# Two-layer graph network on one core: GpSimd's subtraction waits for the tile's one-hots, its unused constants come later, and no filler matmuls stand between the picks

## The chip, the cores and the metric
The kernel runs on one core of a Trainium2 chip. The core has a matmul engine (TensorE, PE), a vector engine (VectorE, DVE), an activation engine (ScalarE, ACT), a general engine (GpSimd, POOL), and SyncE (SP), whose queue starts the DMAs here. Each engine works through its own list of instructions in order, and semaphores tie the lists together. The metric is the device time of the one launch in microseconds (us); the value of a kernel is the median of its runs.

## The reference
There are 3125 nodes with 256 features and 50000 edges (`src`, `dst`, sorted by `dst`).

```python
# layer 0: mean over the edges of each row, twice, on the same edges
vals  = 1 / max(deg(rows), 1)
neigh = segment_sum(vals[:, None] * x[cols], rows)
x     = relu(concat([x, neigh], 1) @ W.T + b)            # W0,b0 then W1,b1
# outer: x = layernorm(x + two such layers)
# layer 1: the 32 largest of x @ W_neigh are kept per node and averaged over the edges
x     = layernorm(x + (x @ W_self + segment_sum(maxk(x @ W_neigh)[src], dst) / max(deg, 1)[:, None]))
```

Weights, biases and edges are inputs; nothing of them is known when the kernel is built.

## The kernel before, in words
The kernel turns the edge list into a dense matrix C of 3125 x 3125 edge counts, in 25 x 25 blocks of 125 x 125, and then every segment sum is a matmul with C or its transpose.

**Start.** ScalarE turns the edge numbers into floats. VectorE finds the last destination of each chunk of edges (`ends`, helper `whole_part`, L606 and L607), compares it with a ramp (`before`, L621), splits the edge numbers (L625 to L632) and makes selection masks (`pick`, L637). TensorE multiplies the pieces of the edge numbers with the masks in two rounds (k = 0: the first 125 windows, L1385 on `bank`; k = 1: the other 500, L1385 on `pair`). ScalarE copies the results out (`row`, L1089), VectorE unpacks them (L643 to L649), and ScalarE writes them as `jobs` (L1096). GpSimd meanwhile writes the constants: ramps, ones, identities (L483 to L520).

**Tiles 0 and 1.** VectorE compares a ramp with `jobs` and gets one-hot matrices (`hots`, L665, `quick_hots(t, k)`, four sets to a tile). TensorE multiplies them (`fill(t, f)`, L1406), and ScalarE copies the counts into a slab (L1114). In the same stretch the maxima of the weights are found (L688 is the last part), TensorE transposes them (`bounds_t`, L1447), VectorE reduces the transposed rows (`bound_rows`, L772), TensorE turns these once more (`bounds_row`, L1451), and a chain of small VectorE instructions makes scales from them (`bounds`, L784 to L799; `scales_out`, L803). The product of the node features with the weights (`own_product`, L1520) of tile 1 cannot start before the scales.

**The loop over tiles, t = 1 to 24.** For each tile TensorE does the four fills of tile t, the 25 transposes of tile t - 1 (L1486, in groups g = 0 to 3), two products L1520 and two transposes of node features (L1501). VectorE makes the four one-hots of tile t + 1 and copies two of the groups of transposes out of PSUM (`tr_copy`, L822): one-hot 0, group 1, one-hots 1, 2 and 3, group 3. ScalarE copies the fills (L1114), the other two groups (L1153), the transposed features (L1158) and the product (`own`, L1171). Then GpSimd splits the product's half a0 into two 16-bit parts (`split_a0`): a cast (L544, when `own` is there) and a subtraction (L546, when the cast is done). SyncE stores the slab (L353) and half of the product (L360). In tiles 4 and 5 the weights are split as well (L1176 on ScalarE, L817 on VectorE).

**The rest.** From about 172 us on, three series of 625 big matmuls (L1593 twice, L1689) and the dense products (L1494) follow; the change touches nothing there.

`keep_clock(b, n)` (L1349) issues n matmuls of 512 columns on a tile of ones whose result nobody reads. The numbers of a wait on `const_ready` say how many constants must be written: the list of GpSimd sets which ones these are. A path for edge lists that don't fit the windows (`general_...`) is in the program, but not taken with these inputs. It alone reads `iota16`, `woff`, `inc_f`, `rev_f` and `wcol`.

Of the kernel before, what the change touches and what calls it, by code (L numbers as in the profile page):

```python
# [30 lines left out]
NT = N // P  # L31
CH = E // P
# [6 lines left out]
NW = N // W  # L39
# [6 lines left out]
FILLS = len(SETS)  # L46
# [8 lines left out]
KEY = NT * W  # L55
B0W = 13
EQ, EG = 4, CH // 4
# [21 lines left out]
ACT = mybir.ActivationFunctionType  # L79
# [4 lines left out]
def gnn(nc, x, src, dst, w0, b0, w1, b1, wself, wneigh, out):  # L84
    ctx = ExitStack()
    with ctx:
# [174 lines left out]
        const_ready = sem("const_ready")  # L261
# [220 lines left out]
        def _(pool):  # L482
# [16 lines left out]
            for m, n in ((identf, 128), (ident16, PC), (identx, P)):  # L499
# [4 lines left out]
                           allow_small_or_imprecise_dtypes=True).then_inc(const_ready, 1)  # L504
            nc.gpsimd.memset(ones16[:, :], 1.0).then_inc(const_ready, 1)
            nc.gpsimd.memset(epsy[:, :], EPS / YS ** 2).then_inc(const_ready, 1)
            nc.gpsimd.memset(epsb[:, :], EPS).then_inc(const_ready, 1)
            for i in range(2):
# [3 lines left out]
            nc.gpsimd.iota(iota16[:, :], [[1, KEY]], base=0, channel_multiplier=0,  # L512
                           allow_small_or_imprecise_dtypes=True).then_inc(const_ready, 1)
            nc.gpsimd.iota(woff[:, :], [[KEY, NW]], base=0, channel_multiplier=0,
                           allow_small_or_imprecise_dtypes=True).then_inc(const_ready, 1)
            nc.gpsimd.iota(inc_f[:, :], [[1, EQ], [EQ, EG]], base=1, channel_multiplier=0,
                           allow_small_or_imprecise_dtypes=True).then_inc(const_ready, 1)
            nc.gpsimd.iota(rev_f[:, :], [[-1, EQ], [-EQ, EG]], base=CH, channel_multiplier=0,
                           allow_small_or_imprecise_dtypes=True).then_inc(const_ready, 1)
            nc.gpsimd.iota(wcol[:, :], [[0, 1]], base=0, channel_multiplier=1,  # L520
                           allow_small_or_imprecise_dtypes=True).then_inc(const_ready, 1)
            pool.wait_ge(const_ready, 9)
            pool.wait_ge(ws_loaded, 16)
            for c in range(2):
                w_eye = ws_nat[:, c, c * 128:(c + 1) * 128]
                nc.gpsimd.tensor_tensor(w_eye, w_eye, identf[:, :], ALU.add).then_inc(eye_added, 1)

# [7 lines left out]
            def split_a0(t):  # L535

                pool.wait_ge(own_copied, t + 2)
                if t == 0:
                    pool.wait_ge(scale_ready, 1)
                    nc.gpsimd.tensor_tensor(own[:, 0, :], own[:, 0, :], scales[0:P, 1:2].broadcast_to([P, 2 * F]), ALU.mult  # L540
                                            ).then_inc(own_scaled, 1)
                    pool.wait_ge(own_scaled, 1)
                a0 = own[:, t % 2, F:2 * F]
                nc.gpsimd.tensor_copy(xs[:, t, 0:F], a0).then_inc(a0_hi, 1)  # L544
                pool.wait_ge(a0_hi, t + 1)
                nc.gpsimd.tensor_tensor(xs[:, t, F:2 * F], a0, xs[:, t, 0:F], ALU.subtract).then_inc(a0_split, 1)  # L546
# [43 lines left out]
        NCONST = 23  # L590
# [3 lines left out]
        def _(dve):  # L594
# [100 lines left out]
            dve.wait_ge(const_ready, NCONST)  # L695
# [21 lines left out]
            def general_table():  # L717
# [8 lines left out]
                dve.wait_ge(win_hot, 2 * FILLS)  # L726
                dve.wait_ge(win_done, FILLS)
# [176 lines left out]
            with dve.If(total > E - 1):  # L904
                for t in range(1, NT):
# [3 lines left out]
                    if t == 1:  # L909
                        bound_rows()  # L910
                    if t == 2:
                        dve.wait_ge(cols_copied, 4)
# [141 lines left out]
        def _(act):  # L1054
# [7 lines left out]

            def as_float(j, n):
                a.activation(edges_f[:, j], edges_i[:, j], ACT.Copy).then_inc(floats_ready, 1)
                act.wait_ge(floats_ready, n)
# [112 lines left out]
            def quick_copies():  # L1178
                quick_copy(0, FILLS - 1)
                square_x(3)  # L1180
                for t in range(1, NT):
                    own = OWN[t]
                    quick_copy(t, 0)
                    if t == 1:
                        own_t(0)
                    tr_copy(t - 1, 0)
# [157 lines left out]
        def _(pe):  # L1344
# [30 lines left out]
            for k, (lo, hi) in enumerate(PICKS):  # L1375
                for blk in range(2):
                    out = both[1][:, blk, 0:hi - lo] if k else bank[4][:, blk * hi:(blk + 1) * hi]
                    mm(out, ones_row[:, :], minus_row[:, lo:hi], start=True, stop=False, skip_group_check=True)
                    for g in range(EQ):
# [7 lines left out]
                        if k:  # L1387
                            keep_clock(bank[7], 1)
# [350 lines left out]
```

## Time and profile before
| | us |
|---|---|
| median of 3 runs (lowest, highest) | 659.98 (658.75, 664.8) |
| profiled execution, its own time | 660.82 |
| its span in the profile | 659.0 |
| TensorE busy in the span | 632.4 (96%) |
| VectorE busy | 494.8 (75%) |
| ScalarE busy | 315.4 (48%) |
| GpSimd busy | 111.4 (17%) |
| mean granted TensorE clock | 0.989 of 2.4 GHz |

A busy share is a mean over the whole span, and stages differ: VectorE is busy without a break in the loop over tiles and half idle later on. Times of instructions are counted from the start of the span. An instruction's end is drawn until its result is written, so the next one on the engine can start some 0.1 us before it.

### The profile page before, as it was taken

How to read it: one execution, taken by the hardware profiler on the slowest of the kernel's cores; microseconds unless marked ns; L12 is line 12 of the kernel's file. 1: busy time of each engine (PE TensorE's matmuls, PEld its weight loads, DVE VectorE, ACT ScalarE, POOL GpSimd, SP SyncE). 2: the span in 40 equal slices, each digit the busy share in tenths (PEclk: the TensorE clock that was granted, in tenths of full speed). 3: DMA queues.
4: the chain of work that ended last, by engine and by line, in shares of the span. 5: the costliest groups of instructions: out<-in, count | busy, mean ns of one | idle time of the engine just before them, and what ended most of it. 6: DMA issues, size and time to landing. Idle time of an engine off the chain costs nothing.

```text
span 659.0 us, 10805 instructions
## 1 busy us (share of the span) xinstructions
PE 632.4 (96%) x3758; PEld 322.7 (49%) x3759; DVE 494.8 (75%) x1273; ACT 315.4 (48%) x606; POOL 111.4 (17%) x188
## 2 busy tenths in 40 slices
PE   8879999999999999999998999999999999999996
PEld 3456666776544444444443444444444444444442
DVE  7888999999759998888845588878878837533333
ACT  3678999999397777676622222222222200000000
POOL 3104221221200111001002223232232200000000
PEclk9979999999999999999999999999999999999999
DMA  8534655555522222222224999999999533300000
GB/s 212 109 97 141 225 178 184 186 172 172 160 42 64 59 69 67 53 61 58 51 52 133 189 182 201 180 185 196 174 202 177 154 99 116 111 26 26 24 24 24
DMA packets 66742, 79.62 MB, mean 121 GB/s; under 512 B 30320, under 2 KB 59407, under 8 KB 66681
## 3 DMA queue, kind: packets, MB, share of 16 engines
q1 hardware_dynamic: 66681, 78.86, 55.5%
q8 instruction: 32, 0.52, 0.4%
q14 instruction: 29, 0.24, 0.1%
HBM read 38.91 MB, written 33.38 MB: 110 GB/s over the span
## 4 chain that ended last, share of the span: by engine, by line
PE 63%; DVE 22%; DMA 6%; ACT 4%; POOL 3%; issue 2%; SPq 0%; ACTq 0%; DVEq 0%; POOLq 0%
PE pair L1593 21%; PE bank L1689 11%; PE pair L1689 10%; PE bank L1520 5%; DVE hots L665 4%; PE bank L1486 4%; DMA tr_sb<-part 4%; PE pair L1406 4%; DVE m L985 3%; PE bank L1494 3%; PE pair L1494 3%; DVE work L990 3%; ACT a L1273 2%; POOL part L573 2%; DVE ct L822 1%
## 5 line engine op out<-in xcount | busy, mean ns | idle before, releaser
L1593 PE MATMUL pair<-a,ct 125*128 125x512 f16 x625 | 139.5, 380 | 0.0
L1593 PE MATMUL pair<-xs,ct 125*128 125x512 f16 x625 | 139.1, 379 | 0.0
L665 DVE TENSOR_TENSOR hots<-iota,jobs 125x1792 f16<-125x1792 f16 (+1 forms) x100 | 103.7, 1073 | 0.7 <-ACT jobs L1096 0.7
L1593 PEld LDWEIGHTS pair<-a,ct 125*128 125x128 f16 x625 | 62.3, 100 | 74.6 <-issue 1.4
L1593 PEld LDWEIGHTS pair<-xs,ct 125*128 125x128 f16 x625 | 61.9, 99 | 72.5
L1114 ACT ACTIVATE slab<-pair 125x875 f16<-125x875 f32 (+1 forms) x100 | 83.3, 860 | 3.3 <-PE pair L1406 1.7
L1273 ACT ACTIVATE a<-ct 125x1000 f16<-125x1000 f16 (+1 forms) x75 | 80.4, 1072 | 1.6
L555 POOL TENSOR_TENSOR own_in<-own_in,bias_sb 125x256 f32<-125x256 f32 x50 | 37.6, 752 | 238.5 <-DMA own_in<-own_dram 238.4
L1689 PE MATMUL bank<-xs,ct 125*128 125x512 f16 (+1 forms) x325 | 71.5, 379 | 0.0
L1689 PE MATMUL pair<-xs,ct 125*128 125x512 f16 x300 | 66.2, 379 | 0.0
L1340 ACT ACTIVATE sd<-mv,epsb 125x1 f32<-125x1 f32 x25 | 7.4, 294 | 113.9 <-DVE mv L1047 113.9
L878 DVE SCALAR_TENSOR_TENSOR t<-pair,rdeg,own_in 125x256 f32<-125x256 f32 x50 | 24.1, 482 | 48.0 <-PE pair L1593 43.3
L1486 PEld LDWEIGHTS bank<-ident,slab 125*128 125x128 f16 x625 | 39.6, 99 | 35.9 <-issue 22.1
L1486 PE MATMUL bank<-ident,slab 125*128 125x125 f16 x625 | 51.5, 220 | 4.8 <-ACT slab L1114 1.7
L1406 PE MATMUL pair<-hots 125*128 125x125 f16 x625 | 52.4, 223 | 3.9 <-DVE hots L665 3.0
L1520 PE MATMUL bank<-w_t,x_t 128*125 128x512 f32 x100 | 53.6, 621 | 1.6 <-DVE sv L784 0.9
L1689 PEld LDWEIGHTS bank<-xs,ct 125*128 125x128 f16 (+1 forms) x325 | 32.3, 99 | 37.9
L1689 PEld LDWEIGHTS pair<-xs,ct 125*128 125x128 f16 x300 | 29.9, 100 | 34.9
L1406 PEld LDWEIGHTS pair<-hots 125*128 125x128 f16 x625 | 40.6, 100 | 7.7 <-issue 4.7
L1494 PE MATMUL bank<-w_lay,tr_sb 128*128 128x512 f16 x150 | 37.6, 388 | 4.2 <-DMA tr_sb<-part 4.2
L822 DVE COPY ct<-bank 125x1008 f16<-125x1008 f16 x50 | 33.7, 673 | 7.6 <-PE bank L1486 7.6
L856 DVE TENSOR_TENSOR tree<-tree,ct 125x630 uint16<-125x630 uint16 x75 | 37.5, 500 | 1.8
(203 smaller groups left out, 753.7 us busy)
## 6 DMA issues: line engine op xcount, KB each, us to landing
c_dram<-slab SPq DMA_DIRECT2D x25, 683.6 KB
ct<-c_dram SPq DMA_DIRECT2D x25, 683.6 KB
own_in<-own_dram SPq DMA_DIRECT2D x50, 125.0 KB
own_dram<-own SPq DMA_DIRECT2D x25, 125.0 KB
own_dram<-own_st SPq DMA_DIRECT2D x25, 125.0 KB
x_in<-in_x_dram SPq DMA_DIRECT2D x25, 125.0 KB
z_dram<-z_st SPq DMA_DIRECT2D x25, 125.0 KB
a<-z_dram SPq DMA_DIRECT2D x5, 625.0 KB
```

The costliest lines, as they stand in the source:

```text
L555: nc.gpsimd.tensor_tensor(own_in[k % 2][:, :], own_in[k % 2][:, :], bias_sb[:, :], ALU.add).then_inc(own_biased, 1)
L665: v.tensor_tensor(hots[k][:, :, :, :].rearrange("p w g (a d) -> p (w g) a d", d=2), iota, job, ALU.is_equal).then_inc(win_hot, 1)
L822: v.tensor_copy(ct[:, TG0[g]:TG0[g] + TG[g], t, :], tr16[1][0:P, 0:TG[g], 0:PC]).then_inc(tr_free[1], 1)
L856: step(v.tensor_tensor(tree[:, :], tree[:, :], quint[k], ALU.add))
L1114: a.activation(slab3[t % 2][:, :, lo * QW:hi * QW].rearrange("p b (w d) -> p b w d", d=QW), pair[f % 2][0:P, 0:n, 0:QKEY].rearrange("p w ( ...
L1273: a.activation(unread[:, 0:(hi - lo) * P].rearrange("p (b s) -> p b s", s=P), ct[:, lo:hi, T, 0:P], ACT.Copy, accum_out=deg_part[:, T, k:k ...
L1406: last = mm(pair[f % 2][:, u, 0:QKEY], hots[f][:, u, 0, :], hots[f][:, u, 1, 1:QKEY + 1], start=True, stop=True, skip_group_check=True)
L1486: last = nc.tensor.transpose(tr16[g % 2][:, i, 0:P], slab[par][:, (TG0[g] + i) * P:(TG0[g] + i) * P + 128], ident16[:, 0:P])
L1494: last = mm(out, lhs(2 * pt + h), w[:, h, q, :], start=h == 0 and k == 0, stop=h == 1 and k == 2, skip_group_check=True)
L1520: last = mm(bank[6][0:P, :].rearrange("p (a f) -> p a f", a=2), x_t32[:, h, :], w0_t[:, h::2, :], start=h == 0, stop=h == 1, skip_group_ch ...
L1593: ins = mm(agg[k % 3][0:lhs.shape[1], :], lhs, parts[l][:, t, :], start=t == 0, stop=t == NT - 1, skip_group_check=True)
L1689: ins = mm(out3[T % 8][0:lhs.shape[1], :], lhs, xs[:, b, :], start=b == 0, stop=b == NT - 1, skip_group_check=True)
```

## The change
GpSimd's list of constants is cut in three. The first eleven that count for `const_ready` stay where they were. Seven short ones wait until VectorE has written `row_key` and `row_src` of the first round (`cols_ready` 2). The five that only the general path reads wait until the one-hots of tiles 0 and 1 are done (`win_hot` 8) and count for a semaphore of their own. VectorE's first one-hot waits for 11 constants instead of 23. The two addends of identities (L526 before, L516 now) keep their wait for the weights. In `split_a0` the subtraction of tiles 4 to 23 waits for the four one-hots of tile t + 1. The eight matmuls of ones between the picks of round k = 1 are gone. ScalarE runs one activation of a single element at its start.

```diff
@@ gpsimd
             nc.gpsimd.iota(iota128[:, :], ...).then_inc(const_ready, 1)
+            pool.wait_ge(cols_ready, 2)
             nc.gpsimd.memset(ones16[:, :], 1.0).then_inc(const_ready, 1)
...
             nc.gpsimd.memset(onesq[:, :], 1.0).then_inc(const_ready, 1)
-            nc.gpsimd.iota(iota16[:, :], ...).then_inc(const_ready, 1)
-            nc.gpsimd.iota(woff[:, :], ...).then_inc(const_ready, 1)
-            nc.gpsimd.iota(inc_f[:, :], ...).then_inc(const_ready, 1)
-            nc.gpsimd.iota(rev_f[:, :], ...).then_inc(const_ready, 1)
-            nc.gpsimd.iota(wcol[:, :], ...).then_inc(const_ready, 1)
-            pool.wait_ge(const_ready, 9)
             pool.wait_ge(ws_loaded, 16)
             for c in range(2):
                 w_eye = ws_nat[:, c, c * 128:(c + 1) * 128]
                 nc.gpsimd.tensor_tensor(w_eye, w_eye, identf[:, :], ALU.add).then_inc(eye_added, 1)
+            pool.wait_ge(win_hot, 2 * FILLS)
+            nc.gpsimd.iota(wcol[:, :], ...).then_inc(general_ready, 1)
+            nc.gpsimd.iota(iota16[:, :], ...).then_inc(general_ready, 1)
+            nc.gpsimd.iota(woff[:, :], ...).then_inc(general_ready, 1)
+            nc.gpsimd.iota(inc_f[:, :], ...).then_inc(general_ready, 1)
+            nc.gpsimd.iota(rev_f[:, :], ...).then_inc(general_ready, 1)
@@ split_a0
                 pool.wait_ge(a0_hi, t + 1)
+                if 3 < t < NT - 1:
+                    pool.wait_ge(win_hot, FILLS * (t + 2))
                 nc.gpsimd.tensor_tensor(xs[:, t, F:2 * F], a0, xs[:, t, 0:F], ALU.subtract).then_inc(a0_split, 1)
@@
-        NCONST = 23
+        NCONST = 18
@@ vector
-            dve.wait_ge(const_ready, NCONST)
+            dve.wait_ge(const_ready, 11)
...
                     if t == 1:
                         bound_rows()
+                        dve.wait_ge(general_ready, 5)
@@ scalar
+            act.wait_ge(warm_ready, 1)
+            a.activation(own[0:1, 0, 0:1], warm[0:1, 0:1], ACT.Copy)
...
                     if t == 1:
                         own_t(0)
+                        act.wait_ge(general_ready, 5)
@@ tensor, picks
-                        if k:
-                            keep_clock(bank[7], 1)
```

GpSimd's list before, from the ramp that the one-hots read (`iota`, L503) to the first split; the names after the numbers of lines are the tiles written and read:

```order
L503 IOTA iota_66 125x128
L505 MEMSET ones_52 125x1
L506 MEMSET epsy 125x1
...
L511 MEMSET onesq 125x125
L512 IOTA iota_86 125x625
L514 IOTA woff 125x125
L516 IOTA inc_f 125x400
L518 IOTA rev_f 125x400
L520 IOTA wcol 125x1
L526 TENSOR_TENSOR ws_nat<-ws_nat,identf 128x128 [waits ws_loaded,const_ready]
```

The same place now:

```order
L503 IOTA iota_66 125x128
L506 MEMSET ones_52 125x1 [waits cols_ready]
L507 MEMSET epsy 125x1
...
L512 MEMSET onesq 125x125
L516 TENSOR_TENSOR ws_nat<-ws_nat,identf 128x128 [waits ws_loaded]
L516 TENSOR_TENSOR ws_nat<-ws_nat,identf 128x128
L518 IOTA wcol 125x1 [waits win_hot]
L520 IOTA iota_86 125x625
L522 IOTA woff 125x125
L524 IOTA inc_f 125x400
L526 IOTA rev_f 125x400
```

The stretch behind the ramp starts only when VectorE has unpacked the first round, and the five general constants have moved behind the addends and behind tile 1's one-hots.

VectorE's list now, from tile 1's last one-hots into the loop's first pass:

```order
L668 TENSOR_TENSOR hots_64<-iota_66,jobs 125x1536 [waits win_done]
L688 TENSOR_REDUCE stat<-bcol 128x2 [waits b_loaded]
L691 TENSOR_REDUCE stat<-ws_nat 128x2 [waits eye_added]
...
L668 TENSOR_TENSOR hots_61<-iota_66,jobs 125x1792 [waits win_done]
L777 TENSOR_REDUCE stat_r<-bank 16x1 [waits stat_psum]
L778 TENSOR_REDUCE stat_r<-bank 16x1
L827 COPY ct<-bank 125x8x126 [waits tr_done,general_ready]
```

VectorE's order is the old one. New is the wait for `general_ready` ahead of the first copy of transposes, and that GpSimd's five constants now start when the first of these rows ends.

TensorE's second round of picks now:

```order
L1388 MATMUL pair<-minus_row,ones_row 128x500
L1395 MATMUL pair<-pick,quint 128x500
L1395 MATMUL pair<-pick,piece 128x500 x2
L1395 MATMUL pair<-pick,quint 128x500
L1395 MATMUL pair<-pick,piece 128x500 x2
```

Before, a row `L1349 MATMUL bank<-warm 128x512` stood behind each pair of `quint` and `piece` rows of this round, eight in all.

## Rows read from the trace of the kernel before
**Rows 1.** Stretches: length, busy us of each engine (instructions), granted clock, DMA

```profile
34.40:40.00 5.60, 5.09 (x46) 4.48 (x47) 3.72 (x8) 4.65 (x8) 0.00 (x0) 0.50 0.44 141
40.00:48.00 8.00, 6.20 (x65) 4.51 (x64) 7.52 (x24) 5.98 (x11) 0.04 (x1) 0.99 0.34 101
...
78.00:125.00 47.00, 45.94 (x505) 32.47 (x504) 47.00 (x55) 44.90 (x73) 10.37 (x18) 1.00 0.56 174
...
370.00:600.00 230.00, 226.63 (x1046) 102.33 (x1044) 164.08 (x564) 48.39 (x131) 45.81 (x68) 1.00 0.87 151
```

**Rows 2.** Timeline, start: start us, us, engine, line, operation, tiles [idle <-releaser]

```profile
4.07 0.24 POOL L503 IOTA iota<- 125x128 f16 x1
...
4.18 2.32 DVE L606 TENSOR_SCALAR ends<-ends 100x4 f32<-100x4 f32 x1
...
4.29 1.28 ACT L1064 ACT_TABLE_LOAD   x1 [4.15 <-DMA edges_i<-in_dst_dram]
...
4.73 0.65 POOL L512 IOTA iota<- 125x625 f16 x1
...
6.41 0.13 POOL L520 IOTA wcol<- 125x1 f32 x1
6.53 0.17 DVE L607 TENSOR_SCALAR ends<-ends 100x4 f32<-100x4 f32 x1
6.73 1.91 DVE L621 TENSOR_SCALAR before<-win_row,ends 100x625 f16<-100x625 f32 x4
```

**Rows 3.** Chain that ended last, second round of picks: start us, us, what

```profile
17.88 0.43 PE bank L1349
...
20.55 0.22 PE bank L1349
...
25.28 1.11 ACT row L1089
```

**Rows 4.** Timeline, tiles 0 and 1

```profile
26.41 1.20 DVE L643 SCALAR_TENSOR_TENSOR held_row<-row 125x1000 f32<-125x1000 f32 x1 [1.49 <-ACT row L1089]
...
32.97 1.80 DVE L665 TENSOR_TENSOR hots<-iota,jobs 125x1536 f16<-125x1536 f16 x2
...
35.38 1.09 DVE L665 TENSOR_TENSOR hots<-iota,jobs 125x1792 f16<-125x1792 f16 x1
...
36.85 0.27 DVE L773 TENSOR_REDUCE stat_r<-bank 16x1 f32<-16x128 f32 x1
...
37.59 0.21 PE L1451 MATMUL bank<-identf,stat_r 16*1 16x16 f32 x2
```

**Rows 5.** Timeline, one pass of the loop

```profile
103.43 1.07 PE L1520 MATMUL bank<-w_t,x_t 128*125 128x512 f32 x2
...
104.62 0.60 PE L1486 MATMUL bank<-ident,slab 125*128 125x125 f16 x8
...
105.33 0.40 POOL L544 CAST xs<-own 125x256 f16<-125x256 f32 x1 [4.00 <-ACT own L1171]
105.39 0.67 DVE L822 COPY ct<-bank 125x1008 f16<-125x1008 f16 x1
105.48 0.38 ACT L1158 ACTIVATE x_t<-bank 128x250 f32<-128x250 f32 x1 [0.21 <-PE bank L1501]
...
105.81 0.67 POOL L546 TENSOR_TENSOR xs<-own,xs 125x256 f16<-125x256 f32 x1
...
105.99 1.31 DVE L665 TENSOR_TENSOR hots<-iota,jobs 125x1536 f16<-125x1536 f16 x1
...
108.08 0.95 DVE L665 TENSOR_TENSOR hots<-iota,jobs 125x1536 f16<-125x1536 f16 x1
```

**Rows 6.** Timeline of GpSimd's casts and a store's wait in the loop

```profile
73.56 0.90 POOL L544 CAST xs<-own 125x256 f16<-125x256 f32 x1 [4.83 <-ACT own L1171]
...
87.38 0.93 ACT L1114 ACTIVATE slab<-pair 125x875 f16<-125x875 f32 x1 [0.43 <-DMA c_dram<-slab]
...
167.41 0.40 POOL L544 CAST xs<-own 125x256 f16<-125x256 f32 x1 [4.00 <-ACT own L1171]
```

More of the change, by code:

```diff
@@ L258, in gnn @@
         out3 = [bank[i] for i in (7, 2, 0, 1, 5, 6, 3, 4)]
-        const_ready = sem("const_ready")
+        const_ready, general_ready = sem("const_ready"), sem("general_ready")
         src_loaded, dst_loaded, dst_more = sem("src_loaded"), sem("dst_loaded"), sem("dst_more")
@@ L511, in _ @@
             nc.gpsimd.memset(onesq[:, :], 1.0).then_inc(const_ready, 1)
[L512 to L521, printed above, removed]
-            pool.wait_ge(const_ready, 9)
             pool.wait_ge(ws_loaded, 16)
@@ L526, in _ @@
                 nc.gpsimd.tensor_tensor(w_eye, w_eye, identf[:, :], ALU.add).then_inc(eye_added, 1)
+            pool.wait_ge(win_hot, 2 * FILLS)
+            nc.gpsimd.iota(wcol[:, :], [[0, 1]], base=0, channel_multiplier=1,
+                           allow_small_or_imprecise_dtypes=True).then_inc(general_ready, 1)
+            nc.gpsimd.iota(iota16[:, :], [[1, KEY]], base=0, channel_multiplier=0,
+                           allow_small_or_imprecise_dtypes=True).then_inc(general_ready, 1)
+            nc.gpsimd.iota(woff[:, :], [[KEY, NW]], base=0, channel_multiplier=0,
+                           allow_small_or_imprecise_dtypes=True).then_inc(general_ready, 1)
+            nc.gpsimd.iota(inc_f[:, :], [[1, EQ], [EQ, EG]], base=1, channel_multiplier=0,
+                           allow_small_or_imprecise_dtypes=True).then_inc(general_ready, 1)
+            nc.gpsimd.iota(rev_f[:, :], [[-1, EQ], [-EQ, EG]], base=CH, channel_multiplier=0,
+                           allow_small_or_imprecise_dtypes=True).then_inc(general_ready, 1)
             steps = [3]
@@ L726, in general_table @@
                 dve.wait_ge(win_hot, 2 * FILLS)
+                dve.wait_ge(general_ready, 5)
+                dve.sem_inc(win_hot, FILLS * NT)
                 dve.wait_ge(win_done, FILLS)
@@ L910, in _ @@
                         bound_rows()
+                        dve.wait_ge(general_ready, 5)
                     if t == 2:
```

## The prediction
> **What bounds the kernel now.** I read the page first, then the stretches, then the timelines of the stretches that the change touches. TensorE is busy 96% of the span, but that is a mean. From 370 us on it is busy 226.63 of 230 us and nothing there is changed [rows 1]. So the change can only move the moment at which the series of big matmuls begins, and whatever it moves there reaches the end in full. Ahead of it lie two stages with other limits.
>
> In the start a chain runs from the edge list through VectorE, TensorE's two rounds of picks and VectorE again. The odd row is L606: 2.32 us for 100x4 elements, where L607, the same kind on the same tile, takes 0.17. L606 ends at 6.50, and GpSimd, which issued constants without a break, ends its last one at 6.54 [rows 2]. So VectorE was held until GpSimd stopped.
>
> In the loop over tiles VectorE is busy 47.00 of 47.00 us, ScalarE 44.90 [rows 1]. VectorE binds. One of its four one-hots takes 1.31 us where an equal one takes 0.95: 0.36 more. It starts at 105.99 beside GpSimd's subtraction, which runs from 105.81 to 106.48 and keeps its 0.67 [rows 5]. The cast at 105.33 lies beside VectorE's copy out of PSUM, and neither is stretched. A pass takes (167.41 - 73.56) / 18 = 5.21 us [rows 6].
>
> **Constants out of the early chain.** GpSimd's last instruction ahead of its new wait is the ramp of L503, which ends at 4.31 [rows 2]. L606 then ends about there, L607 runs 4.36 to 4.53, and L621 can start at 4.56 instead of 6.73: 2.17 us earlier. Bounds: 0, if something else held L606, and 2.2, if it is not held at all. I take 2.17, as the two ends coincide within 0.04. What follows is VectorE's own work up to the picks, so the shift holds. The seven short constants now come after `row_src` of the first round, while VectorE waits for ScalarE's `jobs`; they lay between 4.31 and 4.73 before [rows 2], so 0.4 us at most; beside a wait I put nothing. VectorE's first one-hot waits for fewer constants: nothing, they were long there. ScalarE's table load, 1.28 us from 4.29 [rows 2], moves ahead of the edges' arrival; VectorE wants the first floats after L621's 1.91 us, in the changed kernel at 6.47, 0.9 us after the table load's old end at 5.57, and then works on the first for three instructions; nothing either.
>
> **The ones between the picks.** Eight matmuls at 0.43 each, as the first, are 3.4 us; at 0.22, as a later one [rows 3], 1.8. The clock rises early in the round, so I take 2.1 us on the chain. They can't bring all of it. VectorE reads the second round's copy at 26.41 after 1.49 us of idleness, so it was ready at 24.92 [rows 4]; 2.17 earlier that is 22.75. TensorE's side gives 25.28 - 2.17 - 2.10 = 21.0, with the copy's 1.11 then 22.1. VectorE is late by then, and L643 starts at 22.75: 26.41 - 22.75 = 3.66 us for both edits together. The bounds are 2.17 (the ones bring nothing) and 4.27 (all of both).
>
> **General constants after tile 1's one-hots.** These last one-hots end at 34.77 [rows 4], less 3.66 is 31.11. GpSimd then works from about 31.17 through its five constants, 6.54 - 4.73 = 1.81 us [rows 2], to 32.98. VectorE wants the next one-hot (before at 35.38, so at 31.72) and is held as at L606: 1.26 us. The two reductions behind it, which ended at 37.12, would be awaited at 37.59 [rows 4], by TensorE's L1451; they had 0.17 us of idleness before them and 0.47 behind. 1.26 - 0.17 - 0.47 = 0.6 us late, on the chain to the scales. Bounds: 0, and 1.26. The new waits for `general_ready` on VectorE and ScalarE come later than 32.98 and cost nothing. So the loop is entered 3.66 - 0.6 = 3.06 us earlier.
>
> **The subtraction.** It now starts when the fourth one-hot ends, which is about 0.08 after VectorE's copy (group 3) has started; with the wait's 0.06 it runs from 0.14 to 0.81 of that copy. The next one-hot follows 0.60 after a copy's start [rows 5]. So 0.2 us of overlap is left instead of 0.49. 0.49 cost 0.36, 0.13 less than the overlap, so 0.2 costs 0.05 to 0.09. VectorE's pass loses about 0.3 us. Behind it stand the others. TensorE's eight transposes start at 104.62, 0.12 after the product's drawn end at 104.50; they waited for VectorE's copy, and ScalarE's L1158 idled 0.21 for TensorE [rows 5]. ScalarE's idle time is (47.00 - 44.90) / 9 = 0.23 us to a pass [rows 1]. With VectorE 0.3 faster ScalarE and TensorE's order become the limit, and I take 0.23 us to a pass, with ends at 0.12 and 0.31. 18 passes: 4.1 us (2.2 to 5.6). Queued behind the waiting subtraction is only the next tile's cast, some 1.4 us later; ScalarE's `own` waits for the subtraction two tiles back. Both are free. Tiles 4 and 5 are bound by ScalarE, which also splits weights there; nothing.
>
> **Sum.** 3.06 + 4.1 = 7.2 us. Against the profiled execution's own time of 660.82 that is 653.6; the median of the runs is 0.84 lower, so **652.8**. The terms' bounds give 650.3 to 655.6 for this case.
>
> **Rivals.** (1) *The loop is bound elsewhere already.* Once ScalarE waited 0.43 us in it for a slab's store to land [rows 6]; if stores or ScalarE's order take over at once, 0.05 us or less to a pass is left: 3.06 + 0.9, 656. Against it: only one such wait in 18 passes. (2) *The low clock stays.* The first of the ones took 0.43, a later one 0.22 [rows 3]: the granted clock rose from 1.2 to 2.4 GHz during this dense round, after TensorE had waited for VectorE. With nothing between the picks it could rise only later. 26 matmuls at 0.43 are 11.2 us from 13.9, to 25.1: 0.2 us instead of 3.66, and a gain of 0.2 - 0.6 + 4.1 = 3.7, 656.3. Against it: the picks are back to back, so TensorE is no less busy without the ones. After the branch the clock was 0.50 for 5.6 us, and 0.99 in the next 8 with 6.20 us of work [rows 1]; where it falls there shifts the entry by up to 1 us either way. The Trainium skill (TensorE: Matmul & The Clock Gate, What's actually happening) says that the gate is closed by default and that activity opens it. By that rule filler between dense matmuls adds no activity, and the first term stays; the rise in the trace inside the dense round agrees. (3) *Slower: the subtraction holds the copy.* In its new place it lies beside a copy out of PSUM for 0.45 us; the trace shows one only where the first copy's last 0.25 us runs beside it (105.81 against 106.06 [rows 5]). If each copy is held for the full 0.67, a pass changes by 0.67 - 0.36 = +0.31, 5.6 us in all, less 3.06: +2.5, 662.5. It decides from 0.53 us to a pass on. Against it: the cast beside the copy stretches nothing. The Trainium skill (GPSIMD Reference, Specifications) names contention for VectorE instructions in a 2-port mode or with two SBUF inputs; the copy reads PSUM, so by that rule it isn't held, the one-hot with two SBUF inputs is, and the sum is mine. No row here shows a whole subtraction beside a copy. (4) *L606 was not held by GpSimd*, the edit doesn't do what it says: then 1.49 (VectorE's idleness, filled by the ones' 2.1) - 0.6 + 4.1 = 5.0, 655.
>
> **Chances.** Forecast 0.60; (1) 0.13; (2) 0.10; (3) 0.04; (4) 0.05; both terms at their upper ends or more, 650 or below, 0.08. The range reaches from the lower bound to (2): 650.0 to 656.5. A change of 1% is about what can be told from none: 653.4 and 666.6 are the lines. The forecast lies only 0.6 us inside the first, so I put six tenths of its chance below, with the last case 0.44, and 0.03 more for a low clock that falls away altogether: faster 0.47, within 1% 0.50, slower 0.03.
>
> **What would show it.** L606 at about 0.2 us and L621 starting at 4.6. L643 of the second round at 22.8 with no or little idle time before it. Five constants at 31 to 33 and a one-hot of 2 us or more beside them. In the loop, four one-hots of 1.08 and 0.95 us, the subtraction beside a copy of unchanged 0.67, a pass of 4.98, and ScalarE without idle time before L1158. L1520's products after the scales 3.1 us earlier. It is wrong if the loop's pass stays at 5.15 or more, if the clock is low for longer in the first 50 us, or if TensorE waits anew after the branch.

## The result, and the profile after

| | before | after |
|---|---|---|
| median of 4 runs, us (lowest, highest) | 660.53 (658.75, 664.8) | 652.61 (652.33, 653.37) |
| ratio, 95% interval | | 0.9882 (0.9842 to 0.9923) |
| profiled execution, its own time | 660.82 | 652.5 |
| its span | 659.0 | 650.7 |
| TensorE, VectorE, ScalarE busy | 632.4, 494.8, 315.4 | 624.4, 487.2, 314.8 |

The forecast was 652.8. The change makes the kernel 1.2% faster, with an interval that reaches from 0.8% to 1.6%. The medians differ by 7.92 us. The profiled executions differ by 8.32 us. Three instants cut this sum: the cast of tile 6 comes 3.85 us earlier (73.56 to 69.71), the 18 passes behind it take 3.99 us less, and 0.48 us is gained behind the cast of tile 24. That last piece is within the scatter: from this cast to the end the profiles of the network kernels below take 490.3 to 492.0 us, with the same instructions there.

The timeline of the changed kernel's start answers [rows 2]; L609, L610 and L624 are L606, L607 and L621 of before.

```profile
4.07 0.24 POOL L503 IOTA iota<- 125x128 f16 x1
4.18 0.17 DVE L609 TENSOR_SCALAR ends<-ends 100x4 f32<-100x4 f32 x1
4.39 0.17 DVE L610 TENSOR_SCALAR ends<-ends 100x4 f32<-100x4 f32 x1
4.59 1.91 DVE L624 TENSOR_SCALAR before<-win_row,ends 100x625 f16<-100x625 f32 x4
```

The instruction that took 2.32 us takes 0.17, and L624 starts 2.14 us earlier.

The next rows, from the timelines of GpSimd, ScalarE, VectorE and TensorE, answer [rows 4]. L646 is L643 of before, L668 is L665, L1459 is L1451.

```profile
19.97 1.10 ACT L1098 ACTIVATE row<-pair,shift 125x1000 f32<-125x1000 f32 x1 [0.84 <-PE pair L1395]
22.49 1.19 DVE L646 SCALAR_TENSOR_TENSOR held_row<-row 125x1000 f32<-125x1000 f32 x1
...
31.01 0.67 POOL L520 IOTA iota<- 125x625 f16 x1
31.47 1.09 DVE L668 TENSOR_TENSOR hots<-iota,jobs 125x1792 f16<-125x1792 f16 x1
32.27 0.48 POOL L526 IOTA rev_f<- 125x400 f32 x1
...
33.66 0.21 PE L1459 MATMUL bank<-identf,stat_r 16*1 16x16 f32 x2
```

ScalarE's row copy comes 5.31 us earlier and VectorE's L646 3.92, now without idle time. The ramps for the general path run from 31.01 to 32.75, beside the whole of the one-hot at 31.47, and it takes 1.09 us as before. L1459 is 3.93 us earlier: nothing was given back between the two.

The stretches of the changed kernel, in the columns of [rows 1]: the picks, the branch, the work behind it, the loop, and the matmuls at the end.

```profile
13.90:19.80 5.90, 5.90 (x29) 2.48 (x28) 4.89 (x13) 4.32 (x7) 0.82 (x8) 1.00 1.14 218
28.00:30.00 2.00, 0.00 (x0) 0.00 (x0) 2.00 (x5) 0.34 (x2) 0.00 (x0) 0.63 0.00 0
30.00:36.00 6.00, 5.02 (x49) 4.34 (x49) 4.06 (x8) 5.05 (x8) 1.83 (x5) 0.55 0.42 132
...
78.00:125.00 47.00, 46.33 (x525) 34.28 (x525) 46.77 (x57) 46.20 (x76) 11.81 (x20) 1.00 0.60 188
361.70:591.70 230.00, 226.66 (x1048) 103.02 (x1046) 164.43 (x565) 48.28 (x131) 45.88 (x68) 1.00 0.84 151
```

The picks run at the full granted clock, where the kernel before had 0.51 from 16.2 to 19.6, in these rows of its timeline and stretches:

```profile
13.92 0.21 PE L1385 MATMUL bank<-pick,quint 100*128 100x125 f16 x1 [1.13 <-DVE pick L637]
...
16.20:19.60 3.40, 3.40 (x9) 1.18 (x9) 2.44 (x7) 3.40 (x6) 0.67 (x2) 0.51 1.13 256
```

Behind the branch the clock is at 1.2 GHz as before. In the loop ScalarE went from 44.90 of 47.00 us to 46.20, and VectorE from 47.00 to 46.77. TensorE's busy time at the end is that of before, 226.66.

One pass of the loop, and behind the dots the casts of tiles 6 and 24 and a copy between them, from the timelines of the engines, answer [rows 5] and [rows 6].

```profile
98.08 0.67 DVE L827 COPY ct<-bank 125x1008 f16<-125x1008 f16 x1
98.30 0.67 POOL L549 TENSOR_TENSOR xs<-own,xs 125x256 f16<-125x256 f32 x1 [2.73 <-DVE hots L668]
98.67 1.25 DVE L668 TENSOR_TENSOR hots<-iota,jobs 125x1792 f16<-125x1792 f16 x1
...
100.43 2.68 DVE L668 TENSOR_TENSOR hots<-iota,jobs 125x1536 f16<-125x1536 f16 x3
...
69.71 0.40 POOL L545 CAST xs<-own 125x256 f16<-125x256 f32 x1 [1.45 <-ACT own L1180]
82.70 0.93 ACT L1123 ACTIVATE slab<-pair 125x875 f16<-125x875 f32 x1 [0.69 <-DMA c_dram<-slab]
159.57 0.40 POOL L545 CAST xs<-own 125x256 f16<-125x256 f32 x1 [0.97 <-ACT own L1180]
```

The subtraction lies beside the copy for 0.45 us, and the copy keeps its 0.67. The subtraction's last 0.30 us lies beside the next one-hot, which takes 1.25. The other three take 2.68 together. A pass is (159.57 - 69.71) / 18 = 4.99 us.

### The profile page after: what moved, and what is told of

The parts are those of the page before. It is cut to its first block, busy times and chain, and to the rows that moved or that the text cites. A ratio compares the mean times of both kernels' runs of the same rounds, so it can differ in the third digit from the quotient of the medians.

```text
span 650.7 us, 10811 instructions
## 1 busy us (share of the span) xinstructions
PE 624.4 (96%) x3750; PEld 322.3 (50%) x3751; DVE 487.2 (75%) x1273; ACT 314.8 (48%) x607; POOL 111.3 (17%) x188
## 4 chain that ended last, share of the span: by engine, by line
PE 50%; DVE 19%; ACT 17%; DMA 5%; issue 4%; POOL 3%; SPq 0%; ACTq 0%; DVEq 0%; POOLq 0%
PE pair L1601 21%; PE bank L1697 11%; PE pair L1697 10%; ACT slab L1123 8%; DVE m L991 4%; DVE work L996 3%; PE bank L1502 3%; DMA tr_sb<-part 3%; PE pair L1502 3%; ACT ct L1162 2%; POOL part L576 2%; ACT own L1180 2%; ACT a L1283 2%; DVE hots L668 2%; POOL xs L580 1%
## 5 line engine op out<-in xcount | busy, mean ns | idle before, releaser
L668 DVE TENSOR_TENSOR hots<-iota,jobs 125x1792 f16<-125x1792 f16 (+1 forms) x100 | 99.0, 1025 | 0.8 <-ACT jobs L1105 0.8
```

What stands on the lines that cost most here:

```text
L668: v.tensor_tensor(hots[k][:, :, :, :].rearrange("p w g (a d) -> p (w g) a d", d=2), iota, job, ALU.is_equal).then_inc(win_hot, 1)
```

## Experiments

Times are medians. A ratio is to the kernel before, in runs on the same chip. "Cast 0", "cast 6" and "cast 24" are GpSimd's casts of these tiles; before they start at 49.07, 73.56 and 167.41.

### The three parts, each alone

**e1_consts**: the kernel before with only the constants moved, and the waits on them that go with it.

```diff
+            pool.wait_ge(cols_ready, 2)
             nc.gpsimd.memset(ones16[:, :], 1.0).then_inc(const_ready, 1)
...
-            nc.gpsimd.iota(iota16[:, :], ...)   # and woff, inc_f, rev_f, wcol
...
+            pool.wait_ge(win_hot, 2 * FILLS)
+            nc.gpsimd.iota(iota16[:, :], ...).then_inc(general_ready, 1)   # and the other four
```

> The kernel before with the constants' move alone (the ones between the picks and the old subtraction stay). Theory A, GpSimd's stream of constants holds L606: L606 takes 0.17 us instead of 2.32, the chain to the second picks moves by 2.2 us, VectorE still idles for the picks, and the launch gains 2.2 us, 1.9 to 2.6 (about 658 against 660.5). Theory B, L606 is slow by itself and the start's gain of the full change came from the ones: L606 stays at 2.3, gain 0 to 0.3. For the five general constants: if they hold the one-hot beside them, that one-hot takes 2 us or more and the gain is only 1.6; the changed kernel's trace speaks for 1.09 us and no loss.

Measured: 657.7, ratio 0.9963 (0.9944 to 0.9982). L607 (L606 before) takes 0.17 us at 4.18. Rows of ScalarE's, VectorE's and GpSimd's timelines and the stretch of the picks:

```profile
21.51 1.10 ACT L1092 ACTIVATE row<-pair,shift 125x1000 f32<-125x1000 f32 x1 [3.00 <-PE pair L1389]
22.64 1.20 DVE L644 SCALAR_TENSOR_TENSOR held_row<-row 125x1000 f32<-125x1000 f32 x1
45.39 1.15 POOL L545 CAST xs<-own 125x256 f16<-125x256 f32 x1
...
13.90:21.60 7.70, 7.70 (x39) 3.30 (x37) 6.69 (x15) 4.41 (x8) 2.23 (x9) 1.00 1.13 225
```

With the ones still between the picks, cast 0 comes 3.68 us earlier. Of the 3.66 that I had shared out between the constants and the ones, the constants alone bring all: the clock does not fall in the picks any more, and VectorE's 1.49 us of idleness goes with that. Theory A had L606 right and this wrong: it expected VectorE to go on idling. The medians differ by 2.34 us, as expected, but the profiled executions by 3.58. The 3.68 us are those of the profiles, and how many of the other executions have them is not shown.

**e2_ones**: the kernel before with only the ones taken out.

```diff
-                        if k:
-                            keep_clock(bank[7], 1)
```

> The kernel before without the eight matmuls of ones, nothing else changed. Theory A: TensorE ends the second picks 1.8 to 2.1 us earlier, VectorE's idle time of 1.49 us before L643 vanishes and bounds the gain: 1.4 to 1.5 us. Theory B, without the ones the granted clock stays at 1.2 GHz for longer: the picks of 500 columns take 0.43 us to the end and the gain is 0 or a loss of up to 2 us. Theory C, the picks gain all of 2.1.

Measured: 660.07 (657.11 to 665.17), ratio 0.9991 (0.9964 to 1.0019).

```profile
16.20:25.30 9.10, 9.10 (x22) 2.92 (x22) 6.84 (x15) 4.02 (x7) 0.93 (x2) 0.50 0.80 176
...
4.39 3.78 DVE L621 TENSOR_SCALAR before<-win_row,ends 100x625 f16<-100x625 f32 x4
26.48 1.10 ACT L1089 ACTIVATE row<-pair,shift 125x1000 f32<-125x1000 f32 x1 [6.26 <-PE pair L1385]
27.61 1.20 DVE L643 SCALAR_TENSOR_TENSOR held_row<-row 125x1000 f32<-125x1000 f32 x1 [3.33 <-ACT row L1089]
51.70 1.15 POOL L544 CAST xs<-own 125x256 f16<-125x256 f32 x1
```

This is my rival (2), on its own. TensorE is busy for all of the 9.10 us, and the granted clock is 0.50 throughout: VectorE waits 3.33 us instead of 1.49, and cast 0 is 2.63 us late. The profiled execution took 662.6, 2.5 more than the median, so not every execution pays this much. But no gain was found either. One more reading: L606 began 0.24 us earlier here (3.94) and took 0.21, L607 took its 0.17 at 4.18, and the hold fell on L621, 3.78 us for 1.91. So the hold is tied to no single instruction, and to no single instant either: at 4.18 L606 was held in the kernel before, and L607 was not held here.

**e3_sub**: the kernel before with only the subtraction's wait.

```diff
                 pool.wait_ge(a0_hi, t + 1)
+                if 3 < t < NT - 1:
+                    pool.wait_ge(win_hot, FILLS * (t + 2))
```

> The kernel before with the subtraction's wait alone. Theory A: a pass of the loop takes 4.96 to 5.0 us instead of 5.21, 18 passes bring 3.9 to 4.1 us, the launch gains 4 (about 656.5). The one-hot behind the copy keeps 0.17 us of stretch. Theory B, the loop's gain needed an earlier start (other landings of the stores): under 3 us, with ScalarE waiting for stores more than once. If the three parts are independent, their gains (2.2, 1.5, 4.0) add up to 7.7 against 7.9 measured for all.

Measured: 655.41, ratio 0.9925 (0.9896 to 0.9953).

```profile
73.14 0.40 POOL L544 CAST xs<-own 125x256 f16<-125x256 f32 x1 [1.44 <-ACT own L1174]
162.62 0.40 POOL L544 CAST xs<-own 125x256 f16<-125x256 f32 x1 [1.02 <-ACT own L1174]
```

A pass is 4.97 us instead of 5.21. Cast 6 is 0.42 earlier, and so is cast 0 by 0.41, ahead of the first tile that the edit touches, so that this is scatter of the start. The whole gain of the loop comes from this wait. The product of the ratios of e1 and e3 is 0.9888, that of the full change 0.9882.

### What GpSimd's work does to VectorE's

**m1_table** leaves the network out and runs groups of four VectorE instructions beside eight of GpSimd's.

> Not the network: only a table of what GpSimd's work does to VectorE's. Five kinds of VectorE work, four of each back to back (scalar on 32-bit data, comparison of two 16-bit tiles as in the one-hots, copy out of PSUM, reduction, three-operand instruction with two SBUF inputs) stand beside five of GpSimd's (nothing, ramps, memsets, casts, subtractions, eight of each back to back). Theory A, one lock for everything: each of VectorE's SBUF kinds is held by each of GpSimd's until its stream ends. Theory B, it depends on the pair: ramps and memsets, which only write, hold the one-input scalar kind (L606) but not the comparison (0.95 us stays), while the subtraction, which reads, holds the comparison (0.3 us or more each); the copy out of PSUM and the reduction are held by none (0.67 stays). The changed kernel's trace speaks for B: its one-hot beside the ramps took 1.09.

The rows are VectorE's timeline. The order is: beside nothing (from 4.21), beside ramps (17.64, 24.01), beside subtractions (from 92.85).

```profile
4.21 1.67 DVE L73 TENSOR_SCALAR d_ts<-a 125x625 f32<-125x625 f32 x4 [0.16 <-POOLq L88]
6.04 3.56 DVE L75 TENSOR_TENSOR d_eq<-iota,jobs 125x1536 f16<-125x1536 f16 x4 [0.15 <-POOLq L93]
...
17.64 3.20 DVE L73 TENSOR_SCALAR d_ts<-a 125x625 f32<-125x625 f32 x4 [0.15 <-POOLq L93]
24.01 3.56 DVE L75 TENSOR_TENSOR d_eq<-iota,jobs 125x1536 f16<-125x1536 f16 x4 [3.17 <-POOLq L108]
...
92.85 4.98 DVE L75 TENSOR_TENSOR d_eq<-iota,jobs 125x1536 f16<-125x1536 f16 x4 [3.20 <-POOLq L108]
101.04 2.45 DVE L77 COPY d_cp<-ps 125x1008 f16<-125x1008 f16 x4 [3.21 <-POOLq L108]
```

All of it, in us for four:

| VectorE | alone | ramps | memsets | casts | subtractions |
|---|---|---|---|---|---|
| scalar, one SBUF input | 1.67 | 3.20 | 3.27 | 2.27 | 3.09 |
| one-hot, two SBUF inputs | 3.56 | 3.56 | 3.56 | 4.16 | 4.98 |
| three-operand, two SBUF inputs | 2.50 | 2.50 | 2.50 | 3.09 | 3.92 |
| copy out of PSUM | 2.45 | 2.45 | 2.45 | 2.45 | 2.45 |
| reduction | 2.47 | 2.46 | 2.46 | 2.46 | 2.46 |

So ramps and memsets, which read nothing, hold the scalar kind alone; casts and subtractions hold also what has two SBUF inputs; copies out of PSUM and reductions are never held. The Trainium skill (SBUF — State Buffer, SBUF: two separate sides) gives a rule for it: the two engines share one pair of ports as a lock, which a VectorE instruction with two SBUF inputs contends for only against a GpSimd operation that reads SBUF. The table agrees in both rows with two SBUF inputs.

**d4_more**: the kernel before with four more ramps of 400 in front of its general constants.

```diff
+            nc.gpsimd.iota(cover[:, :], [[1, CH]], ...)   # and cover2, cover3, cover4
             nc.gpsimd.iota(iota16[:, :], ...)
```

> The kernel before with four more ramps of 400 (0.47 us each, 1.9 in all) on GpSimd right ahead of its general constants. Theory A (VectorE's one-input instruction is held until GpSimd's stream of constants ends): L606, 2.32 us before, grows by as much as the stream, to 4.1 to 4.3, and L607 starts near 8.4 instead of 6.53. Theory B (a fixed cost at the start, or a hold by the first constants alone): L606 stays at 2.3. If its edges land 0.2 earlier the hold may fall on L621 instead.

Measured: 660.45 in its one run.

```profile
4.18 4.00 DVE L614 TENSOR_SCALAR ends<-ends 100x4 f32<-100x4 f32 x1
8.11 0.13 POOL L528 IOTA wcol<- 125x1 f32 x1
...
8.00:14.00 6.00, 4.98 (x16) 2.06 (x17) 5.76 (x13) 0.86 (x3) 0.24 (x2) 0.72 1.13 238
14.00:25.30 11.30, 11.30 (x73) 5.90 (x72) 10.29 (x22) 6.52 (x11) 0.93 (x2) 1.00 1.03 198
```

The first instruction (L614 is L606) grows with the stream, from 2.32 to 4.00, and the stream by 1.70: the hold is GpSimd's doing. What I had not foreseen is the rest. With VectorE 1.68 us later from there on, the second round's unpacking starts at 26.47 against 26.41, and cast 0 at 49.16 against 49.07. The clock is low from 10.2 to 13.7 us, ahead of the picks, and full in them. So in this profile the hold was 1.7 us longer for nothing: what set the end of the start in the kernel before was the low clock in the picks.

### TensorE's clock

**d3_moved** asks whether the second round needs its ones, or only a TensorE that was busy ahead of it. The 8 ones go, and 4 stand in the first round, where TensorE waits for VectorE (the expectation miscounts them as 10 and 5, and so does that of c2_onesback).

```diff
-                        if k:
-                            keep_clock(bank[7], 1)
+                        if k == 0 and blk == 0:
+                            keep_clock(bank[3], 1)
```

> The kernel before with the 10 multiplications of ones taken out of the second round of picks and 5 put into the first, one behind each group of three in its first block, where TensorE waits for VectorE's pick. The constants stay early and no wait is added. Theory A (the clock falls at 16.2 because TensorE worked only 2.14 of the 3.4 us before it, and the second round needs no ones once it has the full clock): clock 1.00 from 14 to 25, ScalarE's row copy of the second round 3 us or more earlier than 25.28, L643 at 22.6 to 24, cast of tile 0 near 45.4 to 47. Theory B (the second round itself loses the clock without its ones, as in e2_ones): clock 0.50 from 16 or 20 on, row copy after 25, cast of tile 0 at 49 or later. Kernel: A 656 to 658, B 660 to 661.

Measured: 658.24, ratio 0.9971 (0.9951 to 0.9991).

```profile
22.51 1.09 ACT L1089 ACTIVATE row<-pair,shift 125x1000 f32<-125x1000 f32 x1 [1.71 <-PE pair L1385]
49.43 1.15 POOL L544 CAST xs<-own 125x256 f16<-125x256 f32 x1
...
24.00:46.00 22.00, 15.25 (x122) 10.75 (x120) 18.30 (x40) 14.61 (x23) 0.00 (x0) 0.69 0.24 76
```

Theory A holds for the picks: the second round runs at full clock (1.00 from 14 to 30) without ones of its own, and the row copy is 2.77 us earlier than in [rows 3]. L643, at 25.21, is 1.20 earlier, short of the 22.6 to 24 that was expected. Theory A's cast 0 was missed: the clock was low from 30.2 to 43.8, where before it was from 33.4 to 40.2, and that took the 1.20 back; the four products L1520 in front of cast 0 took 3.78 us, 1.98 before. The profiled execution was the slowest of the ten (660.07), so most of them need not have had this; the median lies between what the two theories expected.

**c2_onesback**: the changed kernel with the 8 ones put back.

> The changed kernel with the multiplications of ones put back after each group of three in the second round of picks (10 of 0.22 us). Theory A (with the earlier constants' move the clock does not fall any more, and the ones are worth only what the kernel with the constants' move alone shows, 0.16 us at tile 0's cast): ScalarE's row copy moves from 19.97 to about 21.5, VectorE's L648 (the second round's first instruction) from 22.49 to 22.6, cast of tile 0 from 45.23 to 45.4, kernel 652.5 to 653.2. Theory B (my prediction's reason, the ones are 2.1 us on the chain of which 1.5 is a gain at L646): cast of tile 0 moves by over 1 us, kernel 653.8 or more.

Measured: 653.25, ratio 0.9889 (0.9836 to 0.9942); L646 at 22.64 and cast 0 at 45.39, 0.15 and 0.16 us later than without the ones. In the changed kernel they are nearly free: ScalarE's copy ends at 21.07 there, 1.4 us before VectorE wants it, and with the ones just in time. This kernel has ScalarE's early activation and e1_consts has not, and cast 0 is at 45.39 in both, so that the early table load brings nothing there, as predicted.

**c3_filler**: the changed kernel with ones on TensorE behind the product of the hits, where it waits for the branch.

```diff
             last.then_inc(counted, 1)
+            pe.wait_ge(wt_copied, 4)
+            keep_clock(bank[7], 8)
```

> The changed kernel with 8 multiplications of ones (8 of 0.21 us on TensorE) right behind the product of the hits, where TensorE is idle from 27.5 to 30.5 while VectorE copies the match and the engines read it; the granted clock is 0.67 in the idle stretch and near 0.5 from 30.4 to 36. Theory A (the clock fell because TensorE stood idle there, and work in its place keeps it): granted clock near 1.00 from 28 to 34, the transposes L1494 and the picks of tile 1 run at about half their duration, and cast of tile 0 comes 0.3 to 1.0 us earlier than 45.23. Theory B (the work behind 30.5 is itself too sparse): clock low all the same from 31 on, cast of tile 0 within 0.15 us of 45.23. If the 8 delay TensorE's reading of the match, cast of tile 0 is up to 0.5 us later. The kernel's time: 651.6 to 652.9.

Measured: 651.03 (650.48 to 651.67), ratio 0.9851 (0.9798 to 0.9903).

```profile
27.21 0.24 PE L1428 MATMUL bank<-onesq,hits 125*1 125x1 f32 x4 [2.42 <-DVE hits L658]
27.38 3.48 PE L1359 MATMUL bank<-warm 128*128 128x512 f16 x8
...
29.00:30.00 1.00, 1.00 (x4) 0.39 (x3) 1.00 (x4) 0.06 (x1) 0.00 (x0) 0.50 0.00 0
31.00:32.00 1.00, 0.48 (x7) 0.24 (x4) 1.00 (x2) 1.00 (x1) 1.00 (x4) 1.00 0.57 171
44.26 1.15 POOL L545 CAST xs<-own 125x256 f16<-125x256 f32 x1
```

The eight took 3.48 us, as the clock had fallen as they began, after 2.42 us of idleness; it was back at 1.00 by 31 us, and cast 0 came 0.97 us earlier than in the changed kernel. That is theory A's cast 0. But the ones did not keep the clock, as it had it: they brought it back 4.7 us sooner (at 30.6 for 35.4).

**d1_fill2** puts eight ones ahead of the product too, and both eights into a bank that is free then. **d2_best** adds the gate of c4_eyegate.

```diff
+            pe.wait_ge(win_read, FILLS - 1)
+            keep_clock(bank[0], 8)
             pe.wait_ge(count_ready, 2)
...
             last.then_inc(counted, 1)
+            keep_clock(bank[0], 8)
```

> The changed kernel with 16 multiplications of ones into a bank of pair 0 that is free then: 8 ahead of the product of the hits (once ScalarE has read tile 0's third set, near 25.5; TensorE was idle from 24.8 to 27.2) and 8 behind it. In c3_filler the clock fell at 27.3, before its 8 ones began, so they only brought it back at 30.7. Theory A (the clock falls because TensorE stands idle from 24.8 on): with work from 25.5 it stays at 1.00 through 27 to 30, the 16 take 0.21 us each, and the changed kernel's low stretch of 28 to 34.7 is gone; cast of tile 0 at 44.0 to 44.3 (45.23 in the changed kernel, 44.26 in c3_filler), since from 30.7 on both have the full clock; kernel 650.5 to 651.5. Theory B (the gap of 0.7 us and the 1.5 us at the branch are enough to lose it): the clock falls near 28 to 31 again and the cast is at 44.3 to 45.3.

> d1_fill2 and the gate of c4_eyegate together: the pair of one-hots beside the additions falls from 2.08 to 1.82 and VectorE's chain to the second one-hots (no idle in it) is 0.26 shorter. Theory A: cast of tile 0 0.1 to 0.3 us earlier than in d1_fill2. Theory B (ScalarE's wait for the data xs, which was 0.76, 1.17 and less in the runs so far, decides when the first one-hots start and swamps it): no difference beyond 0.4 either way. Kernel 650.2 to 651.5.

Measured: d1 652.15, ratio 0.9893 (0.9864 to 0.9921); d2 652.32, ratio 0.9887 (0.9857 to 0.9917). Two stretches of d1 and one of d2:

```profile
24.00:33.00 9.00, 6.17 (x48) 3.30 (x45) 8.71 (x16) 6.72 (x11) 1.83 (x5) 1.00 0.18 52
33.00:36.00 3.00, 3.00 (x33) 2.71 (x30) 1.61 (x3) 2.46 (x6) 0.00 (x0) 0.50 0.36 127
...
24.00:46.00 22.00, 17.07 (x158) 11.02 (x156) 20.25 (x46) 17.21 (x28) 4.72 (x8) 1.00 0.29 90
```

In d1 the clock survives the branch and falls at 33, which neither theory had; cast 0 is at 44.79, in theory B's range and outside theory A's. In d2 the clock never falls, and cast 0 is at 44.07, the earliest of all and 0.72 before d1's, more than either theory allowed. Both medians lie above what was expected. The two programs differ only in GpSimd's gate. In d2 ScalarE also waited 1.11 us for a load of `xs` ahead of the first eight, in d1 0.29, so that they ran from 25.96 and from 24.99. From 29 to 33 TensorE was then busy for 2.54 us in d2 and for 1.79 in d1. So I can't put the kept clock down to the edit. The table sets the stretch from the second round's unpacking to cast 0 beside the mean granted clock from 24 to 46 us.

| kernel | L643 or L646 | cast 0 | between | clock 24 to 46 |
|---|---|---|---|---|
| d2_best | 22.27 | 44.07 | 21.80 | 1.00 |
| c3_filler | 22.45 | 44.26 | 21.81 | 0.92 |
| d1_fill2 | 22.55 | 44.79 | 22.24 | 0.92 |
| before | 26.41 | 49.07 | 22.66 | 0.84 |
| after | 22.49 | 45.23 | 22.74 | 0.84 |
| e1_consts | 22.64 | 45.39 | 22.75 | 0.84 |
| d4_more | 26.47 | 49.16 | 22.69 | 0.84 |
| d3_moved | 25.21 | 49.43 | 24.22 | 0.69 |

VectorE's and ScalarE's work between the two is the same in all eight but for what GpSimd's work adds, and the stretch follows the clock: 2.4 us from the best to the worst. The other kernels fit: e2_ones took 24.09 us at 0.73, and e3_sub, c1_nosub, c2_onesback and c4_eyegate 22.68 to 22.75 at 0.84.

Against the changed kernel nothing of this is settled by time. c3's ratio to the kernel before is 0.9851 with an interval that holds 0.9882, and those of d1 and d2 are 0.9893 and 0.9887. A gain of 1 us is 0.15%, less than these intervals can tell. What the traces show is an earlier cast 0.

### The rest of the loop and of the start

**c1_nosub**: the changed kernel without the subtraction in tiles 4 to 23.

```diff
+                if 3 < t < NT - 1:
+                    pool.sem_inc(a0_split, 1)
+                else:
                     nc.gpsimd.tensor_tensor(xs[:, t, F:2 * F], ...)
...
```

> This is the changed kernel without the subtraction of tiles 4 to 23 on GpSimd; the first layer's aggregates of those tiles read tile 0's halves instead (that part of the result is left out), and no other instruction is missing. It asks what the 0.17 us that still lie on the one-hot behind the copy (1.25 us there, 1.08 free) cost. Theory A (ScalarE sets the pass now: 89.06 us busy of 89.86 in 18 passes, and VectorE has slack): the pass stays at 4.93 to 4.99 us, the one-hot falls to 1.08, cast of tile 24 within 1 us of 159.57, kernel 651.5 to 652.7. Theory B (VectorE still sets it and the residual stretch is paid): the pass falls by 0.17 to about 4.82, cast of tile 24 near 156.5, kernel near 649.5. The two differ at 156.5 against 159.

Measured: 654.46 (653.41 to 661.05), ratio 0.992 (0.9889 to 0.9952).

```profile
69.94 0.40 POOL L545 CAST xs<-own 125x256 f16<-125x256 f32 x1 [5.62 <-ACT own L1183]
98.31 1.07 DVE L671 TENSOR_TENSOR hots<-iota,jobs 125x1792 f16<-125x1792 f16 x1
159.63 0.40 POOL L545 CAST xs<-own 125x256 f16<-125x256 f32 x1 [5.10 <-ACT own L1183]
```

The one-hot is at its free 1.07 us, and a pass takes 4.98 us all the same. So the 0.17 us that the subtraction still takes from VectorE costs nothing: theory A, VectorE does not set the pass. In the 18 passes ScalarE is busy for 88.74 of 89.69 us and VectorE for 87.66, which points at ScalarE. The median, though, is 1.8 us above what theory A expected, while the profiled execution (653.41) has the stretch behind cast 24 as the others; where the rest went no trace shows. What moves the mean pass now is ScalarE's wait for a slab's store. c2_onesback had three such waits in its loop (0.74, 0.80 and 0.84 us) and a mean pass of 5.07; d2_best had none, and 4.97.

**c4_eyegate**: GpSimd's two additions wait for tile 0's last one-hots.

```diff
+            pool.wait_ge(win_hot, FILLS)
             for c in range(2):
                 w_eye = ws_nat[:, c, c * 128:(c + 1) * 128]
```

> The changed kernel with GpSimd's two additions to the weights (L516, 2.21 us at 19.48) held until tile 0's last one-hots are done (21.3). Now they lie beside two one-hots of VectorE (2.08 us against 1.82 for such a pair). Theory A (reading work of GpSimd holds one-hots and two-input instructions but no reductions): the pair of one-hots falls to 1.82, L646 starts near 22.23 (0.26 earlier) if nothing else holds it; of the additions most lies beside the reductions L679 and L683 (0.67 each, unchanged), and a remainder may stretch L646 (1.19) by up to 0.2. Cast of tile 0 0.1 to 0.3 us earlier than 45.23. Theory B (the stretch of the one-hots is no matter, since ScalarE's L1113 and its row copy set the time): L646 and the cast unmoved within 0.05. The kernel's time stays within 0.5 us either way.

Measured: 653.95, ratio 0.9899 (0.9847 to 0.9951). The pair of one-hots falls from 2.08 to 1.82, as theory A had it. Yet L647 (L646 before) starts at 22.67, 0.18 later: the first one-hots waited 1.16 us for ScalarE's `jobs` instead of 0.75, ScalarE having waited 0.30 us for a load of `xs` that had not held it in the changed kernel. One profile can't part the two. The median is 1.3 us above the changed kernel's, outside the 0.5 that was expected. In d2_best, with the same gate, L647 is at 22.27, 0.28 earlier than in d1_fill2.

## Why the prediction was right, point by point

**L606.** Right: 2.14 us for 2.17, and d4_more shows that GpSimd's stream is the cause.

**The ones, and the entry into the loop.** The size was right: 3.66 predicted for both edits, 3.92 measured at L646. The working was not. I wrote that the ones were 2.1 us on the chain and so filled VectorE's 1.49 us of idleness. e1_consts has the ones and none of the idleness, c2_onesback puts the ones' worth at 0.15 us, and e2_ones has neither ones nor gain. What made the 1.49 was the clock. In the kernel before, TensorE waited 1.13 us for VectorE's first pick, was busy for 2.14 us in all between 12.8 and 16.2, the clock fell then, and the round ran at 0.51 until 19.6. With the constants out of the way VectorE's picks come 2.1 us earlier, TensorE waits 0.23 us for them (e1_consts) or not at all, and the clock stays. The profiles bear this out together: the three kernels with that wait of 1.13 us and nothing in its place (before, e2_ones, e3_sub) lose the clock between 15 and 17 us, and all eight with the constants moved have 1.00 from 8 to 28 us, c3_filler to 27. d3_moved fills the wait and keeps the clock as well. In d4_more the picks come last of all and run at full clock, as TensorE had its low stretch before them; so what counts is not when the picks come. I had read the clock as rising in the round, which it does, and had not asked why it was low at its start. Of the further 0.26, 0.20 is from GpSimd's additions: before they lay beside the first pair of one-hots (2.42 us for 1.96), after beside the second (2.08 for 1.82). That the size came out is luck: both terms were bounded by the same idle time, so the sum was the same whichever of them earned it.

**The general constants.** This step failed: "VectorE wants the next one-hot [...] and is held as at L606". It was put at 0.6 us and cost none. m1_table says why: a ramp reads nothing, and a one-hot beside it keeps its 3.56. I had taken the price from a scalar instruction, which is of another kind.

**The subtraction.** Right: 4.99 us for a pass, 4.98 predicted, and 3.99 us for the 18 against 4.1. The residual on the one-hot is 0.17, not 0.05 to 0.09, but by c1_nosub it is hidden: VectorE is no longer the limit. The step that named the next limit, ScalarE and TensorE's order, held that far; which of the two it is was not tested.

**The sum.** 7.2 predicted, 8.32 in the profiles: 0.8 more at the entry (0.6 that did not occur, and the 0.26), 0.1 less in the loop, and 0.5 behind it, which is scatter. The forecast of 652.8 lies 0.2 from the median although the sum is 1.1 short, because I took 0.84 off between the profiled execution and the median, and for the changed kernel the median lies 0.1 above. That closeness is luck. The stated bounds of 650.3 to 655.6 are also not quite those of the terms: with 1.26 us lost on the general constants the slow end is 659.98 - (2.17 - 1.26 + 2.2), 656.9. Nothing hung on it.

**The rivals.** (1), the loop bound elsewhere, is true only beyond 4.98. (2), the low clock, is real for the ones alone (in the profile of e2_ones), and is kept off by the other edit. I held against it that the picks are back to back, so TensorE was no less busy without the ones; e2_ones has it busy 9.10 of 9.10 us at 0.50, so that argument was worth nothing. (3), the copy held by the subtraction: 0.67 before and after, and 2.45 in all of m1_table's columns. (4) is refuted by e1_consts and d4_more.

## What to carry to other kernels

Before you price an instruction's hold from a row, match three things: whether GpSimd's operation reads SBUF, how many SBUF inputs VectorE's has, and whether it reads PSUM. Before you price the removal of work on TensorE, look at the granted clock of the stretch and at what TensorE did ahead of it: the low stretch here went when TensorE no longer idled ahead of it (e1_consts, d3_moved), and in the profile of e2_ones it was longer with work taken out. And when two edits are capped by the same idle time, run each alone: the sum is right whichever of them earns it.

## What the runs showed of the hardware that was not expected

- A hold can fall on different VectorE instructions: 2.32 us on L606 (starting at 4.18), but 3.78 for 1.91 on L621 in e2_ones, where L606 started at 3.94 and took 0.21. What picks the one isn't shown.
- The hold until the end of GpSimd's stream (4.00 us in d4_more) isn't what m1_table shows: there four scalar instructions took 3.20 us beside ramps that went on for 6.09, and those eight ramps take 4.91 beside one-hots. Both engines were slowed. What makes the one case or the other wasn't found.
- GpSimd pays as well: its eight subtractions take 5.05 us beside copies out of PSUM and 7.99 beside one-hots.
- After TensorE stood idle for 2.42 us in c3_filler, the granted clock fell within the first of the matmuls that followed. In d1_fill2 it outlived the branch and fell at 33, with TensorE busy for 1.79 us from 29 to 33; in d2_best, with 2.54, it did not fall. The Trainium skill (TensorE: Matmul & The Clock Gate, What's actually happening) has the clock follow how busy TensorE has been. These cases fit that. The picks of e2_ones do not: there 9.10 us of unbroken work did not bring the clock up. Why is open.
